# Four buffers in place of two for the halves of h and their transposes in the operand stage of a graph attention kernel

## The reference, cut to what matters

```python
x = _layernorm(x + _L0_gnn_ref(x, adj, ...))
mask = graph + eye(N) > 0
h = einsum('bnc,hdc->bhnd', x, Wh)                 # 4 heads: 32 pairs of batch and head
scores = where(mask, einsum('...nd,...md->...nm', h, h), -1e16)
out_h = einsum('...nm,...md->...nd', softmax(scores), h) + bh
z = leaky_relu(concat of heads, 0.2)
h2 = einsum('bnk,dk->bnd', z, Wo)                  # second attention layer, 8 instances
out2 = the same attention on h2, + bo; leaky_relu; normalise; * gamma + beta
x = _layernorm(x + out2)
```

## Time and profile before

| | us |
|---|---|
| median of 3 runs | 3285.74 |
| lowest, highest | 3283.33, 3295.19 |
| the profiled execution's own time | 3288.88 |
| its span | 3287.0 |

### The profile page before, as it was taken

One profiled execution on the slowest core, in us unless ns is written; L12 is line 12 of the kernel. 1 busy time (PEld: TensorE's weight loads), 2 busy tenths in 40 slices (PEclk: granted clock), 3 DMA queues, 4 the chain that ended last, 5 costly groups with the idle time before them and its releaser, 6 DMA issues. The chain is left out here.

```text
span 3287.0 us, 124182 instructions
## 1 busy us (share of the span) xinstructions
PE 2949.7 (90%) x49399; PEld 2173.3 (66%) x49399; DVE 2692.0 (82%) x5392; ACT 2273.3 (69%) x2542; POOL 2629.1 (80%) x1463
## 2 busy tenths in 40 slices
PE   5856699999999999999999999999996689999990
PEld 3425577777777777777777777777765556666660
DVE  5764588888888888888888888888877779999997
ACT  2146577777777777777777777777765567777776
POOL 1136598999999999899989999999987878888880
PEclk8989999999999999999999999999998989999995
DMA  5207888999999988998999999989977568988872
GB/s 207 70 1 257 232 159 150 156 171 165 156 161 171 162 157 161 167 164 155 161 165 164 158 160 166 167 156 161 171 123 185 179 141 148 159 154 156 145 135 84
DMA packets 1442513, 514.23 MB, mean 156 GB/s; under 512 B 1359054, under 2 KB 1416844, under 8 KB 1439884
## 3 DMA queue, kind: packets, MB, share of 16 engines
q1 hardware_dynamic: 1442060, 507.32, 80.1%
HBM read 105.27 MB, written 66.06 MB: 52 GB/s over the span
## 5 line engine op out<-in xcount | busy, mean ns | idle before, releaser
L551 POOL TENSOR_TENSOR low<-probs 128x1024 f16<-128x1024 f32 x1280 | 2396.6, 1895 | 331.6 <-ACT probs L829 232.2
L829 ACT ACTIVATE probs<-scores,shifted_max 128x2048 f32<-128x2048 f32 x640 | 1282.5, 2004 | 254.2 <-DVE shifted_max L1038 248.0
L696 PE MATMUL ps<-operands 128*128 128x512 f16 x2560 | 974.4, 381 | 12.9 <-DVE neg_max L1033 7.0
L697 PE MATMUL ps<-operands 128*128 128x512 f16 x2560 | 973.9, 380 | 0.0
L1033 DVE CUSTOM_DVE_ANT_0 scores<-ps,mask 128x1024 f32<-128x1024 f32 x640 | 781.7, 1221 | 207.6 <-PE ps L697 200.0
L842 ACT COPY probsT<-ps 128x1024 bf16<-128x1024 bf16 x640 | 647.4, 1012 | 425.2 <-PE ps L705 421.0
L1033 DVE CUSTOM_DVE_ANT_0 scores<-ps,mask,neg_max 128x1024 f32<-128x1024 f32 x640 | 821.8, 1284 | 132.2 <-issue 83.9
L705 PEld LDWEIGHTS ps<-ident,probs 128*128 128x128 bf16 x10240 | 650.7, 98 | 408.2 <-issue 240.9
L705 PE MATMUL ps<-ident,probs 128*128 128x128 bf16 x10240 | 781.7, 219 | 46.0 <-DVE probsT L1045 39.3
L715 PE MATMUL ps<-v_parts,probsT 128*128 128x64 f16 x10240 | 684.7, 193 | 1.3 <-issue 1.3
L716 PE MATMUL ps<-v_parts,probsT 128*128 128x64 f16 x10240 | 685.1, 193 | 0.0
(11 more groups left out here) (144 smaller groups left out, 1829.9 us busy)
## 6 DMA issues: line engine op xcount, KB each, us to landing
operands<-hT_d SPq DMA_DIRECT2D x40, 512.0 KB, 4.5
operands<-hT_d SPq DMA_DIRECT2D x80, 256.0 KB, 4.4
v_parts<-h_d SPq DMA_DIRECT2D x40, 512.0 KB, 4.4
probsT<-low SPq DMA_TRANSPOSE x1280, 3.6
z_d<-outs SPq DMA_DIRECT2D x38, 512.0 KB, 3.2
scores<-in_adj SPq DMA_DIRECT2D x16, 1024.0 KB, 4.8
h_d<-probs SPq DMA_DIRECT2D x32, 512.0 KB, 3.5
hT_d<-probs SPq DMA_DIRECT2D x32, 512.0 KB, 2.8
```

What stands on the lines that cost most here:

```text
L551: pool.tensor_tensor(low[:, u, w], probs[:, u, w], high[:, u, w], ALU.subtract).then_inc(sem(f"low{half}"), 1)
L696: pe.matmul(ps[:, b, :], hi_lo[:, p, t * P:(t + 1) * P], hi_lo[:, p, w], start=True, stop=False)
L697: scored = pe.matmul(ps[:, b, :], hi_lo[:, p, t * P:(t + 1) * P], lo_hi[:, p, w], start=False, stop=True)
L829: act.activation(probs[:, 1 - u, :], scores[:, 1 - u, :], ACT.Exp, bias=shifted_max[:, 1 - u:2 - u], scale=-1.0, accum_out=row_sum[:, held ...
```

## The change

`h_parts` and `hT_parts` get four buffers, indexed by w = k mod 4. The four buffers of `h_parts` now fill the whole of `probs`; those of `hT_parts` move into `probsT`, which is unused in this stage. The buffers of x1's parts, of xT and in PSUM stay two, with u = w mod 2. The loop over units (`units`, two steps in a body, two ahead and two behind) is replaced by `quads` (four steps in a body, four ahead and four behind), which the second operand stage has already. The waits of L809, L802 and L1009 are for the store of unit k-4. The stores keep their order and sizes; there are four pairs of semaphores in place of two. In layer 1, `probs` half 0 now held h(28) and h(29), half 1 h(30) and h(31), and `probsT` the four hT: the first tiles' instructions wait for these stores. ACT's exponentials of the first two tiles wait for two h stores each, and the copies into `highT` of tiles 0 and 1 on ACT and DVE wait for one hT store each.

```diff
-        def h_parts(u):
-            return stage16(probs, u, 0, H * G * P)
-
-        def hT_parts(u):
-            return stage16(probs, u, H * G * P, H * G * P)
+        def h_parts(w):
+            return stage16(probs, w // 2, w % 2 * H * G * P, H * G * P)
+
+        def hT_parts(w):
+
+            return probsT[:, w // 2, w % 2].rearrange("p k n -> p (k n)")
...
-        def units(eng, step):
-            step(0, 0)
-            step(1, 1)
-            with strided(eng, 2, UNITS - 2, 2) as k:
-                for u in range(2):
-                    step(k + u, u)
-            step(UNITS - 2, 0)
-            step(UNITS - 1, 1)
...
-        def stores(k, u):
+        def stores(k, w):
+
+            return (k - w) * 4
+
+        def pairs(k, u):
 
             return (k - u) * 8
...
+            def store_h(b, w):
+                sp.wait_ge(sem("p1_lo"), b * 4 + w + 1)
+                sp.dma_start(h_d[:, b * H:(b + 1) * H, w * G * P:(w + 1) * G * P] if isinstance(b, int) else
+                             h_d[:, bass.ts(b, H), w * G * P:(w + 1) * G * P],
+                             h_parts(w).rearrange("p (h n) -> p h n", h=H)).then_inc(sem(f"h_stored{w}"), 16)
+
+            def store_hT(b, w):
+                sp.wait_ge(sem("p1_hT_a"), b * 4 + w + 1)
+                sp.wait_ge(sem("p1_hT_b"), b * 4 + w + 1)
...
             def serve_units(b):
...
+                for w in range(4):
+                    store_h(b, w)
+                    store_hT(b, w)
...
-            for u in range(2):
-                sp.wait_ge(sem(f"h_stored{u}"), 8 * (UNITS - NT // G))
-                sp.wait_ge(sem(f"hT_stored{u}"), 8 * (UNITS - NT // G))
+            for w in range(4):
+                sp.wait_ge(sem(f"h_stored{w}"), 4 * (UNITS - 4))
+                sp.wait_ge(sem(f"hT_stored{w}"), 4 * (UNITS - 4))
             for k in range(OPERAND_DMAS):
                 load_part(0, 0, k)
             serve_units(B - 1)
             for k in range(OPERAND_DMAS):
                 load_part(1, 1, k)
...
-            units(pe, p1_step)
-            turn_h(UNITS - 1, 1)
+            quads(pe, p1_step)
+            turn_h(UNITS - 1, 3)
...
-            def copy_hT(k, u):
+            def copy_hT(k, w):
                 act.wait_ge(sem("p1_hT"), k + 1)
-                since(act, sem(f"hT_stored{u}"), stores(k, u))
-                act.copy(hT_parts(u)[:, 0:2 * G * P], banks16(6, 1)).then_inc(sem("p1_hT_a"), 1)
...
+                since(act, sem(f"hT_stored{w}"), stores(k, w))
+                act.copy(hT_parts(w)[:, 0:2 * G * P], banks16(6, 1)).then_inc(sem("p1_hT_a"), 1)
...
                 since(act, sem("p1_hT"), k - 1)
-                since(act, sem(f"h_stored{u}"), stores(k, u))
-                act.copy(by_tiles(h_parts(u), 0), products(u)).then_inc(sem("p1_hi"), 1)
+                since(act, sem(f"h_stored{w}"), stores(k, w))
+                act.copy(by_tiles(h_parts(w), 0), products(u)).then_inc(sem("p1_hi"), 1)
...
                     if isinstance(i, int) and i == 0 and t <= 2:
-                        act.wait_ge(sem(f"h_stored{t - 1}"), 8 * UNITS)
-                        act.wait_ge(sem(f"hT_stored{t - 1}"), 8 * UNITS)
+                        act.wait_ge(sem(f"h_stored{2 * t - 2}"), 4 * UNITS)
+                        act.wait_ge(sem(f"h_stored{2 * t - 1}"), 4 * UNITS)
...
                 if back(2):
+                    if isinstance(i, int) and i == 0 and t <= 3:
+                        act.wait_ge(sem(f"hT_stored{t - 2}"), 4 * UNITS)
```

More of the change, by code:

```diff
@@ L337, in _ @@
                 sp.dma_start(shifted[lo + 1:hi + 1, BD:2 * BD], h_lo[lo:hi, (NT - 1) * BD:NT * BD]).then_inc(sem("shifted_in"), 16)
-            def serve_units(b):
[L341 to L352, removed]
+            def store_h(b, w):
[6 more added lines that the diff above has]
+                sp.wait_ge(sem("p1_hT_b"), b * 4 + w + 1)
+                sp.dma_start((hT_d[b * H * P:(b + 1) * H * P, w * G * P:(w + 1) * G * P] if isinstance(b, int) else
+                              hT_d[bass.ts(b, H * P), w * G * P:(w + 1) * G * P]).rearrange("(h q) n -> q h n", h=H),
+                             hT_parts(w).rearrange("p (h n) -> p h n", h=H)).then_inc(sem(f"hT_stored{w}"), 16)
+            def serve_units(b):
+                for w in range(4):
+                    store_h(b, w)
+                    store_hT(b, w)
             with sp.Fori(0, B - 1) as b:
@@ L375, in _ @@
                 load_part(1, 1, k)
-            for u in range(2):
-                sp.wait_ge(sem(f"h_stored{u}"), 8 * UNITS)
-                sp.wait_ge(sem(f"hT_stored{u}"), 8 * UNITS)
+            for w in range(4):
+                sp.wait_ge(sem(f"h_stored{w}"), 4 * UNITS)
+                sp.wait_ge(sem(f"hT_stored{w}"), 4 * UNITS)
             def store_z(i, p, base=0):
@@ L647, in turn_x1, with turn_h @@
                 last.then_inc(sem("p1_xT"), 1)
-            def turn_h(k, u):
+            def turn_h(k, w):
                 pe.wait_ge(sem("p1_lo"), k + 1)
@@ L654, in turn_h, with p1_step @@
                 for c in range(H * G):
-                    last = pe.transpose(banks16(6, 2)[:, c * P:(c + 1) * P], h_parts(u)[:, c * P:(c + 1) * P], ident_h[:, :])
+                    last = pe.transpose(banks16(6, 2)[:, c * P:(c + 1) * P], h_parts(w)[:, c * P:(c + 1) * P], ident_h[:, :])
                 last.then_inc(sem("p1_hT"), 1)
-            def p1_step(k, u):
+            def p1_step(k, w, b):
+                u = w % 2
                 pe.wait_ge(sem("p1_xT_copied"), k + 1)
@@ L669, in p1_step @@
                 if within(k - 1):
-                    turn_h(k - 1, 1 - u)
+                    turn_h(k - 1, (w + 3) % 4)
             pe.wait_ge(sem("x1_done"), NT)
             turn_x1(0, 0)
-            units(pe, p1_step)
-            turn_h(UNITS - 1, 1)
+            quads(pe, p1_step)
+            turn_h(UNITS - 1, 3)
             def tile_step(g, i, t, p, back, second):
@@ L812, in p1_step @@
                 if within(k - 1):
-                    copy_hT(k - 1, 1 - u)
+                    copy_hT(k - 1, (w + 3) % 4)
             copy_xT(0, 0)
-            units(act, p1_step)
-            copy_hT(UNITS - 1, 1)
+            quads(act, p1_step)
+            copy_hT(UNITS - 1, 3)
             def tile_step(g, i, t, p, back, second):
@@ L863, in p2_step @@
                 since(act, sem("p2_turned"), k - 1)
-                since(act, sem(f"h2_stored{u}"), stores(k, u))
+                since(act, sem(f"h2_stored{u}"), pairs(k, u))
                 act.copy(h2_part(u, 0), ps[:, 4 + u, 0:G * D].rearrange("p (s d) -> p s d", s=G)).then_inc(sem("p2_hi"), 1)
@@ L1004, in _, with copy_hT, p1_step @@
                 variance(i)
-            def copy_hT(k, u):
+            def copy_hT(k, w):
                 dve.wait_ge(sem("p1_hT"), k + 1)
-                since(dve, sem(f"hT_stored{u}"), stores(k, u))
-                dve.tensor_copy(hT_parts(u)[:, 2 * G * P:4 * G * P], banks16(7, 1)).then_inc(sem("p1_hT_b"), 1)
-            def p1_step(k, u):
+                since(dve, sem(f"hT_stored{w}"), stores(k, w))
+                dve.tensor_copy(hT_parts(w)[:, 2 * G * P:4 * G * P], banks16(7, 1)).then_inc(sem("p1_hT_b"), 1)
+            def p1_step(k, w, b):
+                u = w % 2
                 dve.wait_ge(sem("p1_hi"), k + 1)
-                dve.tensor_tensor(by_tiles(h_parts(u), 1), products(u), by_tiles(h_parts(u), 0), ALU.subtract).then_inc(sem("p1_lo"), 1)
+                dve.tensor_tensor(by_tiles(h_parts(w), 1), products(u), by_tiles(h_parts(w), 0), ALU.subtract).then_inc(sem("p1_lo"), 1)
                 if within(k - 1):
-                    copy_hT(k - 1, 1 - u)
-            units(dve, p1_step)
-            copy_hT(UNITS - 1, 1)
+                    copy_hT(k - 1, (w + 3) % 4)
+            quads(dve, p1_step)
+            copy_hT(UNITS - 1, 3)
             def tile_step(g, i, t, p, back, second):
@@ L1039, in tile_step @@
                 if back(2):
+                    if isinstance(i, int) and i == 0 and t <= 3:
+                        dve.wait_ge(sem(f"hT_stored{t - 2}"), 4 * UNITS)
                     dve.wait_ge(sem("turned0"), g - 1)
@@ L1106, in copy_h2T @@
                 dve.wait_ge(sem("p2_turned"), k + 1)
-                since(dve, sem(f"h2T_stored{u}"), stores(k, u))
+                since(dve, sem(f"h2T_stored{u}"), pairs(k, u))
                 dve.tensor_copy(h2T_parts(u), banks16(6 + u, 1)[:, 0:G * P]).then_inc(sem("p2_hT"), 1)
```

## The result

The changed kernel takes 3315.77 us (median; 3311.02 to 3321.07) against 3285.74 us: 1.0089 times the time before, interval 1.0067 to 1.0112. It is 30 us slower where 29 us faster was forecast. Its profiled execution took 3321.07 us, span 3319.2.

The account below looks back on a forecast made before the run. It took the operand stage to be bound by a two-buffer circle of store latency, not by rate or an engine. Gain 33.1 - 4.0 = 29.1 us from 3288.88 gives 3259.8, on the median's scale 3257; range 3250 to 3273 us.

Parts of the forecast that it names:

- Waits for stores: Operand stage: ACT's 43.2 us of waits for h stores leave the path, with 3.5 us left over across four units.
- What is late next: Operand stage: each cast then waits for its own unit's products; 2.80 us a unit, bounds 2.71 (DMA) to 3.2.
- the chain: Operand stage, one cast hi to the next: cast to xT copy 0.91, to first product 0.65, products 1.05, ACT's wake-up; 2.80 us.
- The term of the wake-up: Operand stage: ACT's cast starts 0.19 us after its unit's products end.
- the share of 358 GB/s: Operand stage stores: at a core's share of its memory domain a unit would take 2.93 us; measured 387 GB/s spoke against it.
- the rival of hindered stores: Operand stage: stores hinder each other, the DMA leads at 3.0 to 3.2 us a unit; 3262 to 3267 us, chance 0.15.
- The last batch: Stage's end: the 10.1 us wait goes wholly; loads issued at 334.0 us start layer 1 at 342.9, 33.1 us earlier.
- Queue behind it: Layer 1's start: tile 0's transposes wait behind stores and loads, slipping 1.7 to 5.1 us; 4.0 taken.
- exp(1)'s wait for h(31): Layer 1's second exponential waits for the last h store, until about 351 us; a slip under 1 us.
- Sum up to here: Whole kernel: 33.1 us earlier start less 4.0 us slip gives a gain of 29.1 us.
- Code: Operand stage: twelve steps of a unit in place of six, three bodies entered once each; nothing, at most 3 us.
- The rival "slower": Operand stage: more stores in flight sink the DMA rate to 229 GB/s, 26 us more; 3312 us, chance 0.05.

Follow-up runs that it names:

- 155 instructions: Changed kernel plus 155 already-met waits in TensorE's program ahead of the operand stage, placing layer 1's code two 256-instruction blocks behind the kernel before: 3264.01 us, ratio 0.9929.
- 101: Kernel before, otherwise untouched, plus 101 instructions of already-met waits in TensorE's program where it idles ahead of the operand stage: 3357.83 us, ratio 1.0206.
- 256: Changed kernel plus 256 instructions of already-met waits, a whole block, in TensorE's program ahead of the operand stage: 3311.94 us, ratio 1.0073.
- 200: Changed kernel plus 200 instructions of already-met waits in TensorE's program ahead of the operand stage: 3309.12 us (one execution).
- 60 instructions: Changed kernel plus 60 instructions of already-met waits in TensorE's program ahead of the operand stage: 3287.41 us (one execution).
- 80: Changed kernel plus 80 instructions of already-met waits in TensorE's program ahead of the operand stage: 3291.77 us in one execution, then 3283.05 us, ratio 0.9994.
- 230: Changed kernel plus 230 instructions of already-met waits in TensorE's program ahead of the operand stage: 3304.28 us (one execution).
- 100: Changed kernel plus 100 instructions of already-met waits in TensorE's program ahead of the operand stage: 3262.26 us, ratio 0.9929.

## Why the prediction was wrong

*Waits for stores.* Right: 43.2 us to 0.6, and in their place short waits for the products.

*What is late next.* 2.80 us a unit was forecast from the chain; hi(2) is at 251.31 and hi(28) at 321.30 us, 2.69 us each, just under the lower end of 2.71. The term of the wake-up, 0.19 us, was too large: in this unit the cast starts 0.03 us after the products end (285.23 + 1.05); in others it is 0.19.

```profile
285.23 1.05 PE L666 MATMUL ps<-w,scores 128*128 128x256 f16 x8
...
286.31 1.01 ACT L811 CAST probs<-ps 128x1024 f16<-128x1024 f32 x1 [0.16 <-PE ps L666]
```

The units thus ask the DMA for 1.049 MB in 2.69 us, 390 GB/s, and it gave this, from 300 to 325 us:

```profile
300.00:325.00 25.00, 21.60 (x265) 17.98 (x266) 16.41 (x19) 23.19 (x29) 20.52 (x28) 1.00 1.09 384
```

This core stored at 384 GB/s for 25 us on end, so the share of 358 GB/s that the prediction took from the Trainium skill ("HBM Reference", "Specifications (TRN2)") did not bind here, and the rival of hindered stores fell.

*The last batch.* Right in mechanism. SP issued the loads 9.89 us after hi(28) and not 5.94: the DMA was behind by then, and hT(27) took 6.8 us and not 2.86 to land (324.38 to 331.19). Against that the faster units gave 2.8 us, and the stage began earlier (hi(2) by 4.0 us, of which layer 0 gave 3.4), so the forecast 342.9 us met the measured 339.79 partly by luck. Counted from hi(0), the first scores come after 95.2 us in place of 128.0: 32.8 us earlier, where 33.1 was forecast.

*Queue behind it.* Right in mechanism, and about right in size in the changed kernel: its first 16 tiles, which lie ahead of the loop, take 66.6 us, before 62.8; the slip is 3.8 us, and TensorE's waits for the transposes are 3.4 (4.0 was taken). The exponential of tile 16 is at 411.58 us, 443.12 before; less layer 0's 3.4 us the change had gained 28.1 us by then. In other placements the slip is larger. With 155 instructions exp(0) is at 346.65 us (380.32 before, 33.7 earlier), and the first 16 tiles take 70.7 us. Of these 7.9 us TensorE's wait for the transposes is 4.9. The term that is too small there is exp(1)'s wait for h(31), put at under 1 us: exp(1) comes 5.43 us after exp(0), before 2.90, a slip of 2.5. There:

```profile
352.08 2.00 ACT L833 ACTIVATE probs<-scores,shifted_max 128x2048 f32<-128x2048 f32 x1 [3.34 <-DMA h_d<-probs]
```

I had added neither this wait nor the DMA's backlog at the loads, which pushes all eight stores back.

*Sum up to here.* With the placement of before the gain is 24.8 us by the spans of the two profiles (3287.0 and 3262.2) and 23 by medians, for the 29.1 forecast; the 3.9 us of slip more in that run are most of the difference.

*Code.* This is the step that failed. The prediction put "nothing" for twelve steps in place of six, with 3 us as the bound, and looked for the price only where the new code runs. The price was paid by old code behind it, 13 times: 57 us at the back edges of a loop that the diff doesn't touch, and the range held no case of it. The rival "slower" was about DMA rates; its time, 3312 us, came near the measured one for a wrong reason. The trace of before did hold a sign. At 2416.36 us, where layer 1's loop is left, stands a wait of 4.01 us for "issue", the same as in the run with 155 (L708, above):

```profile
2416.36 0.93 PE L705 MATMUL ps<-ident,probs 128*128 128x128 bf16 x7 [4.01 <-issue]
```

A transfer of code begins at 2413.16 us, 3.2 us before it ends. So code that isn't there in time costs 4 us at this very loop, and 13 back edges without such a wait were a favourable placement and no property of the loop. The Trainium skill ("Runtime: NRT & Kernel Launch", "Instruction fetch mechanics") says of taken branches that they can wait for such a fetch, and the waits at the back edges agree; I weighed another rule. Priced by this row it would have given a rival with bounds of 0 and 13 x 4 = 52 us on the other side, near the 57 measured.

*Open.* The waits at the back edge follow the remainder by 256, shown by the runs with 101, 155 and 256, and they end with transfers of code. What decides when such a transfer begins isn't known: how head and end give 1.8 + 1.7, 1.8, 0 and 3.6 us is told in part only from 200 to 256, by what is lacking of one fetch; that 60 instructions keep the full 1.8 us and 80 lose it, isn't explained. What the hint does to it, no run shows, nor why transposes land later with 80.

## What to carry to other kernels

Whoever adds or removes code ahead of a long loop moves that loop within the blocks of its code; look for "issue" waits that repeat once per round at the loop's head, and compare a change with an insert of idle instructions of the same length before believing either sign. Here a gain of 23 us was hidden under 52 us of bad placement, and 155 idle instructions gave it back. Transfers on the queue for code, 2 to 3 us ahead of the end of such a wait, tell it from other idle time. Where a trace shows one wait of this kind at a loop's exit, price the same wait at every back edge as a rival.

## What the runs showed of the hardware

At a back edge of a loop that has a hint for the branch's target: two waits of 1.4 to 1.8 us on average (2.0 at most), or one of 1.8 (60 instructions), 2.95 (230) or 3.6 (200), or none over 0.3 (80, 100, 155). In the changed kernel they end 2.4 to 3.0 us after a transfer of 16 KB of code began; where it began 3.2 us ahead or more (80, 100 and 155 instructions, and before) there was none. Where layer 1's loop is left: 4.01 us (before), 3.96 with 155, 1.7 with 60 and with 80. Leaving the operand stage's loop costs 4.58 us with 155, 3.91 with 200 and 3.79 with 230, and nothing that the trace shows in the changed kernel or with 60 or 100. With 155:

```profile
331.65 0.53 PE L645 MATMUL ps<-ident_h,scores 128*128 128x128 f16 x4 [4.58 <-issue]
```

At the sixth back edge of the changed kernel two idle gaps of 1.79 and 1.76 us, ending at 1357.07 and 1360.12 us, were followed by a granted clock of 0.50, the lower level. Stores of 512 KB kept 384 GB/s while all other engines worked.
